# One-hots of the low source digits, eight items per comparison, their cells interleaved

## The reference

```
for W, b in ((W0, b0), (W1, b1), (W2, b2)):        # L0
    h   = x * out_norm[:, None]
    agg = segment_sum(h[src], dst, 12500)
    x   = elu((agg * in_norm[:, None]) @ W + b)
x = layernorm(x0 + x)
msg = relu(x[src] + edge_attr_16 @ W_edge.T + b_edge)   # L1
h   = (x + segment_sum(msg, dst)) @ W1.T + b1
h   = relu(gamma * (h - mean) * rsqrt(var + eps) + beta)
x = layernorm(x + h @ W2.T + b2)
```

## Time and profile before

| | us |
|---|---|
| median of three runs | 6883.4 |
| the profiled execution | 6869.1 |
| its span, first to last instruction | 6867.2 |
| PE busy | 5447.8 |
| DVE busy | 5154.5 |
| POOL busy | 3526.2 |
| ACT busy | 2262.5 |

### The profile page before, as it was taken

How to read it: one execution, slowest core, us unless ns; L and a number is a source line. 1 busy time by engine, 2 the same in 40 slices (tenths; PEclk the granted TensorE clock), 3 DMA queues, 4 the chain that set the end, 5 groups by cost and what they waited for, 6 DMA issues and landing times.

```text
span 6867.2 us, 115093 instructions
## 1 busy us (share of the span) xinstructions
PE 5447.8 (79%) x37560; PEld 2978.5 (43%) x37561; DVE 5154.5 (75%) x22422; ACT 2262.5 (33%) x3807; POOL 3526.2 (51%) x3786
## 2 busy tenths in 40 slices
PE   6899976667776669999999999777777777776773
PEld 4344443333333224555555554444444444444442
DVE  4889999999999994555555554677777777676764
ACT  2776765666543110000000111233333333222221
POOL 6500111111211006777777777677777777777770
PEclk9999999999999999999999999888888988878775
DMA  2522222222221018998988999211111111111110
GB/s 76 214 90 97 93 87 92 105 86 104 81 76 54 28 72 274 282 282 279 278 281 277 285 283 297 81 41 41 41 41 41 41 42 40 39 40 40 40 38 21
DMA packets 420947, 823.42 MB, mean 120 GB/s; under 512 B 146377, under 2 KB 247909, under 8 KB 413525
## 3 DMA queue, kind: packets, MB, share of 16 engines
q1 hardware_dynamic: 292324, 708.34, 31.4%
q0 software_dynamic: 113632, 82.11, 5.3%
q10 hardware_dynamic: 14400, 25.61, 1.3%
HBM read 620.48 MB, written 195.25 MB: 119 GB/s over the span
## 4 chain that ended last, share of the span: by engine, by line
PE 34%; POOL 27%; DVE 26%; issue 10%; ACT 1%; PEld 1%; DMA 0%; PEldq 0%; POOLq 0%; ACTq 0%; DVEq 0%
POOL rows_f L1036 26%; PE banks L2077 21%; DVE rows_f L1286 13%; DVE rows_f L1285 10%; PE banks L1999 5%; PE banks L1961 3%; PE banks L1968 1%; ACT wide L1764 1%; PEld banks L2077 1%; PE banks L2052 1%; PE banks L2059 1%; PE banks L2025 1%; PE banks L2309 1%; POOL tmp L913 1%; POOL hid L915 1%
## 5 line engine op out<-in xcount | busy, mean ns | idle before, releaser
L1036 POOL DMA_INDIRECT rows_f<-table,src_key x1875 | 1791.8, 956 | 571.3 <-issue 571.1
L1286 DVE TENSOR_SCALAR rows_f<-rows_f,tmp 128x392 f16<-128x392 f16 (+2 forms) x5625 | 1854.4, 330 | 0.0
L1999 PE MATMUL banks<-rows_f 128*128 128x392 f16 (+1 forms) x6656 | 1234.7, 306 | 519.1 <-DVE rows_f L1286 361.3
L1764 ACT ACTIVATE wide<-banks 128x784 fp8e4<-128x784 f32 x1563 | 1273.0, 823 | 1068.0 <-PE banks L1999 1063.7
L1001 POOL DMA_INDIRECT sorted_recs<-onehot,rows x1280 | 1237.3, 967 | 616.7 <-issue 376.6
L1285 DVE TENSOR_SCALAR rows_f<-iota_win,hid 128x128 f16<-128x128 f16 x5625 | 1468.8, 261 | 76.5 <-PE banks L1999 71.1
L956 POOL DMA_INDIRECT onehot<-edge_runs_dram,rows_f x352 | 365.0, 1037 | 1755.7 <-DVE onehot L1144 1610.2
L2077 PE MATMUL banks<-wide,rows_f 128*128 128x512 fp8e4 (+1 forms) x4900 | 1127.4, 376 | 12.7 <-issue 12.7
L1999 PEld LDWEIGHTS banks<-rows_f 128*128 128x128 f16 x6656 | 563.6, 97 | 1122.7 <-issue 483.9
L2166 PE MATMUL banks<-w_edge_blk,rows 80*128 80x320 f32 x750 | 345.5, 547 | 667.5 <-DVE rows_f L1586 658.1
L1961 PE MATMUL banks<-wide,onehot 128*128 128x392 fp8e4 x3125 | 786.2, 332 | 36.1 <-ACT wide L1764 25.2
(11 more groups left out here) (327 smaller groups left out, 6587.0 us busy)
## 6 DMA issues: line engine op xcount, KB each, us to landing
wide<-counts SPq DMA_DIRECT2D x504, 896.0 KB
counts<-wide SPq DMA_DIRECT2D x50, 3136.0 KB, 10.0
rows_f<-table,src_key POOLq DMA_INDIRECT x1875
sorted_recs<-onehot,rows POOLq DMA_INDIRECT x1280
sorted_recs<-rows SPq DMA_DIRECT2D x24, 640.0 KB
rows<-attr_dram SPq DMA_DIRECT2D x375, 40.0 KB
agg_a<-attr_dram ACTq DMA_DIRECT2D x50, 250.0 KB
agg_b<-attr_dram ACTq DMA_DIRECT2D x50, 250.0 KB
```

Of the source, the lines that this page charges most:

```text
L1036: G.indirect_dma_start(out=g_rows[:, n % ROW_RING, k, :], out_offset=None, in_=table32[:, :], in_offset=bass.IndirectOffsetOnAxis(ap=src_k ...
L1286: last = V.tensor_scalar(key, iota_key[:, 0:item.width * BLOCKS], key_cols[:, n:n + 1], None, ALU.is_equal)
L1764: A.activation(win_counts[o.half % 2][:, :, d0:d0 + o.quads * QUAD].rearrange("p b (q c) -> p b q c", c=QUAD), counted, ACT.Copy, scale=UN ...
L1999: last = M(octet_ps[n % 2][:, q, at:at + cells], lo, key[:, more:more + cells], start=fresh[q], stop=True, skip_group_check=True)
```

## The change

The `lo` one-hots are made for eight items (a lot) at once: one comparison of two half-precision tensors (TENSOR_TENSOR, 128 x 1024) takes the place of eight TENSOR_SCALAR of 128 x 128. One operand is a constant, each of 0..127 eight times; the other is the lot's eight digit columns, repeated 128 times. The result is 128 cells of eight items each: an item's 128 columns lie 8 elements, 16 bytes, apart, and so PE reads the stationary operand. The digits' columns (`lo_cols`) become half precision. The ring of 20 `lo` is now one of three lots, and before a lot DVE waits until PE has used the item 17 before it. The `key` one-hots, the batches and all other engines' programs are as before, but for one more IOTA on POOL for the constant.

```diff
+LOTS, LOT_BUFFERS = 8, 3
+def lot_need(n):
+    last = n - (LOT_BUFFERS - 1) * LOTS - 1
+    return 0 if last < 0 else 1 + next(k for k, b in enumerate(BATCHES) if b.begin <= last < b.end)
...
-        IOTA_AT = LO_AT + RING * P
+        IOTA_AT = LO_AT + LOT_BUFFERS * LOTS * P
-        lo_ring = spare[:, LO_AT:IOTA_AT]
+        lo_ring = spare[:, LO_AT:IOTA_AT].rearrange("p (s j n) -> p s j n", s=LOT_BUFFERS, n=LOTS)
-        lo_cols = hid_row[:, 0:SLOTS]
+        lo_cols = hid_row[:, 0:SLOTS // 2].bitcast(F16)
+        iota_lots = tmp_row[:, SLOTS:SLOTS + P * LOTS // 2].bitcast(F16).rearrange("p (j n) -> p j n", n=LOTS)
...
-            lo = lo_ring[:, unit * P:(unit + 1) * P]
+            lo = lo_ring[:, n // LOTS % LOT_BUFFERS, :, n % LOTS]
...
+            G.iota(iota_lots, [[1, P], [0, LOTS]], base=0, channel_multiplier=0, **exact)
...
+                if n % LOTS == 0:
+                    if lot_need(n):
+                        dve.wait_ge(s_used, lot_need(n))
+                    V.tensor_tensor(lo_ring[:, n // LOTS % LOT_BUFFERS, :, :], iota_lots,
+                                    lo_cols[:, n:n + LOTS].rearrange("p (o n) -> p o n", o=1).to_broadcast([P, P, LOTS]), ALU.is_equal)
                 item, lo, key = slot(n)
-                V.tensor_scalar(lo, iota_win[:, 0:P], lo_cols[:, n:n + 1], None, ALU.is_equal)
                 last = V.tensor_scalar(key, iota_key[:, 0:item.width * BLOCKS], key_cols[:, n:n + 1], None, ALU.is_equal)
```

## The result

The changed kernel takes 6539.28 us (median of 4 runs, 6537.77 to 6541.02), the kernel before in the same comparison 6882.01 (4 runs). The ratio is 0.9502, with a 95% interval of 0.9485 to 0.9518: 342.7 us are gone. The prediction was 6547, with an own range of 6500 to 6610 for the forecast. Four of the experiments (two of the three with short matmuls, the first pair on the plan of widths) were timed together while the chip ran everything slower, the kernel before too (8484.58 us); they are compared with each other alone.

The account below looks back on a forecast made before the run. DVE was taken to bound C and D, PSUM's chain A, and PE B. Gains of 178 (D) and 159 (C) less 1 (IOTA) make 336 us, so 6883.4 becomes 6547 us; own range 6500 to 6610, overall 6500 to 6830.

Parts of the forecast that it names:

- The lot, 0.61 us from start to start: On DVE, one half-precision comparison for eight items takes 0.61 us, replacing eight lo comparisons of 1.30 us together.
- the dear end: Cost of a lot on DVE if half precision gains nothing: 1.22 us of duration, 1.14 from start to start.
- DVE ends last in C and D: Stretches 924 to 1679 and 1679 to 2539 us: DVE is almost always busy, so time off DVE is off the kernel.
- D, -178: Stretch 1679 to 2539 us, 2111 items, nearly all width 4: 264 lots x 0.69 = 182 us, less 4, gives 178.
- the half of width 8: Within stretch 1679 to 2539 us, 130 items in 32 octets: PE becomes last at 1.78 us per octet; less 4 us.
- C, -159: Stretch 924 to 1679 us, width 2, 512 octets: 119 us from 396 octets with ACT scans, 40 from the other 116.
- my surcharge for odd moments: In stretch 924 to 1679 us, ACT's scans of 0.10 us per octet taken for 0.14, as they break into the chain.
- A and B, 0: Stretches 121 to 396 us (width 4, PSUM chain) and 396 to 924 us (width 8, PE bounds): no change.
- L: Time on PE from one load to the next: up to 0.083 us nothing changes; near 0.24 the gain turns to loss.
- The cover I named: DVE's lead of several octets in 121 to 396 us hides a lot; without it, 90 us lost over both early stretches.
- POOL's IOTA, 1 us: POOL's added IOTA of 1024 elements, ahead of the edge fetches, takes 1.0 us and costs 1 us at most.
- Rival 1: PE's 6656 interleaved loads slow down; 6751 us at 0.213 us per load; chance 0.10 still faster, 0.18 slower.

## Why the prediction was right

- **The lot, 0.61 us from start to start.** Measured 0.60 (690 ns of duration, 0.69 forecast). The reason given, innermost steps of one element in all three tensors, was what decides: with a step of 0 the dear end came true, 1215 ns against 1.22 us. The rule of the Trainium skill (VectorE: DVE Perf Modes, "The perf-mode tier table") agrees with the 690 ns; it agrees with the 1215 ns only as the unpacked tier, which the element type alone would not have told.
- **DVE ends last in C and D.** Right for the kernel before. DVE is busy for 99.6% of D after, too; in C it is now almost level with the chain through PSUM.
- **D, -178.** Measured -179.3. Octets of four items went to 1.26 us (forecast 1.28), the half of width 8 from 65.7 to 57.2 (PE's 1.78 forecast, 1.79 measured per octet). A part was right by luck: PE and its chain stand at 1.24 and not at 1.10 in these octets, as the kernel without lots shows, because I left out PE's wait for ACT there. Had the lot come out cheaper, D would not have followed all the way.
- **C, -159.** Measured -169.5. This is the term that was mis-sized: I let the chain with ACT's scans end at 1.12 us per octet. It can do 1.07 (no lots), and 1.09 was reached. The octets with scans gained 130 us where 119 were forecast, those ahead of them 39 (40 forecast). Without lots an octet takes 1.01 us ahead of the scans and 1.07 with them, 0.06 more for scans of 0.10: my surcharge for odd moments was unfounded.
- **A and B, 0.** Measured +6.5. The term put at nothing cost what the loads cost, 5.9 of it (the contiguous read has it back). The reasoning that nothing changes up to L = 0.083 counted only the distance between loads that follow each other; where nothing hides a load, as behind the in-degree bursts, its duration counts, and that has grown by 49 ns. The cover I named, DVE's lead, did hold: with contiguous loads and a lot of 682 ns, B is 528.2 us. With a lot of 1215 ns it is 531.4 in spite of contiguous loads, so it seems that the lead does not cover just any piece.
- **POOL's IOTA, 1 us.** 1.9 us in the trace (first row below), and the first key starts 0.6 us later (at 121.7 us; from 121.2 to 122.6 in the traces of the variants with the same items outside the slower group, so much of that can be scatter). Scaling by elements missed the order of the cells: with the cells by items the same 1024 elements, also counted in two axes, take the forecast 1.0 us (second row). The two differ in the innermost axis, eight elements of one value or 128 that count up.
- **Rival 1.** It looked at the right quantity, whose size is now known: L is 0.061 us, under the 0.083 of the shortest matmul, and a quarter of the 0.24 at which the sign would turn. The cacheline note of the Trainium skill (SBUF — State Buffer, "Door 1: The DMA port swizzle") is borne out in kind: a load whose elements sit alone on their line takes over twice the time of PE, and it was worth 8 us. It does not fit exactly: at 8 bytes, with two elements on each line, the note has full bandwidth, and the trace has 114 ns and 33 where contiguous loads have 97 and at most 26. The 0.213 of a single-precision load, on which the 6751 us of this rival rested, was too dear by a factor of 3.5.
- **The total.** -342.7 between the medians, -336 forecast. C gained 10.5 us more than forecast and D 1.3 more, and A and B lost 6.5 where no loss was forecast, so that two errors of opposite sign partly cancel. By the traces the stage ends 341.7 us earlier; the last 1 us I take for scatter.

POOL's row by form, of the changed kernel and then with the cells by items:

```profile
L944 POOL IOTA tmp<- 128x1024 f16 x1 | 1.9, 1917 | 0.0
```

```profile
L944 POOL IOTA tmp<- 128x1024 f16 x1 | 1.0, 1008 | 0.0
```

## What to carry to other kernels

Merging small instructions paid twice on the vector engine here, once for the fixed part of each and once because the merged operand's innermost axis has a step of one element. Choose the order of cells for the engine that is last, and let the other one read with a step, if its matmuls are longer than a bare interleaved load: that bound can be measured by cutting the matmuls short. The longer load still costs something wherever nothing hides it. And before the next edit of the same kind, leave the work out altogether once: it shows how far the next bound is (here 17 us in C, and 2 us in the first 96 octets of D).

## What the runs showed of the hardware

- A load of a 128 x 128 half-precision stationary operand lasts 97, 114, 146 and 144 ns with elements 2, 8, 16 and 24 bytes apart; matmuls of 49 columns, each with its load, follow each other every 26, 33 and 61 ns at the first three. Duration and distance are two different prices. The distance stayed under the 83 ns of the shortest matmul and cost nothing until the matmuls were cut; the duration cost 47 ns behind each burst of in-degree matmuls, where nothing hid the load.
- With innermost steps of one, the comparison of two half-precision tensors lasts 413, 690 and 952 ns for 512, 1024 and 1536 elements, 0.51 to 0.54 ns for each further element. With one operand's innermost step at zero it lasts 1215 ns for 1024.
- An IOTA of 1024 half-precision elements in two axes takes 1917 ns with the axis of eight equal values innermost, and 1008 ns with the axis of 128 innermost.
